# Two adjacency widenings moved into the last projection group: a graph layer in fp32 on one Trainium2 core

## The reference

```python
Wi, Wj = (W[:, :Din], W[:, Din:])
mi = jnp.einsum('bkd,od->bko', x, Wi)
mj = jnp.einsum('bkd,od->bko', x, Wj)
a = adj.astype(x.dtype)
deg = a.sum(axis=1)
out = deg[None, :, None] * (mi + b) + jnp.einsum('ij,bjo->bio', a, mj)
return layernorm(x + out)          # over the last axis, eps 1e-5
```

## Time and profile before

| | |
|---|---|
| median of 3 runs | 1672.72 us (1672.58 to 1673.87) |
| the profiled execution | 1672.83 us |
| its span, first to last instruction | 1670.8 us |
| TensorE matmuls | 1642.1 us busy, 98% of the span |
| ScalarE | 667.4 us, 40% |
| VectorE | 841.9 us, 50% |
| GpSimd | 504.7 us, 30% |
| mean granted TensorE clock | 0.996 of full speed |

### The profile page before, as it was taken

How to read it: one execution, slowest core, us unless ns; L and a number is a source line. 1 busy time by engine, 2 the same in 40 slices (tenths; PEclk the granted TensorE clock), 3 DMA queues, 4 the chain that set the end, 5 groups by cost and what they waited for, 6 DMA issues and landing times.

```text
span 1670.8 us, 24989 instructions
## 1 busy us (share of the span) xinstructions
PE 1642.1 (98%) x7248; PEld 1354.5 (81%) x7248; DVE 841.9 (50%) x1884; ACT 667.4 (40%) x970; POOL 504.7 (30%) x390
## 2 busy tenths in 40 slices
PE   7999999999999999999999999999999999999998
PEld 5878888788887888878888788887888878888786
DVE  7767754455444444445544444444454445444444
ACT  5665435423354323542345332453225433254321
POOL 2541124311343113431134311443114421144211
PEclk8999999999999999999999999999999999999999
DMA  5666522333223332343322332224322333232432
GB/s 171 192 185 214 184 82 91 123 110 104 81 95 119 113 107 75 100 126 105 97 86 95 123 109 94 91 92 132 107 88 88 100 126 107 82 101 82 126 111 71
DMA packets 102698, 187.26 MB, mean 112 GB/s; under 512 B 11408, under 2 KB 11408, under 8 KB 102672
## 3 DMA queue, kind: packets, MB, share of 16 engines
q1 hardware_dynamic: 84528, 153.92, 29.0%
q10 hardware_dynamic: 18144, 33.04, 6.5%
HBM read 119.80 MB, written 67.11 MB: 112 GB/s over the span
## 4 chain that ended last, share of the span: by engine, by line
PE 96%; ACT 1%; DVE 1%; issue 1%; DMA 0%; ACTq 0%; SPq 0%; DVEq 0%
PE agg_ps L329 56%; PE cross_ps L295 14%; PE main_ps L305 13%; PE main_ps L307 13%; ACT adjT L411 1%; DVE W_lo L478 0%; DMA mi_dram<-mi 0%; ACT mj_hi L399 0%; PE deg_ps L314 0%; DMA mi_in<-in_wt 0%; DVE deg_part L523 0%; DVE W_df L480 0%; DVE mj L475 0%; DVE cross L475 0%; ACT cross L395 0%
## 5 line engine op out<-in xcount | busy, mean ns | idle before, releaser
L329 PE MATMUL agg_ps<-mj_hi,adjT 128*128 128x512 f32 x2048 | 798.0, 390 | 10.6 <-ACT adjT L411 9.3
L329 PE MATMUL agg_ps<-mj_lo,adjT 128*128 128x512 f32 x2048 | 796.9, 389 | 0.0
L411 ACT ACTIVATE adjT<-adjT 128x2048 fp32r (+1 forms) x128 | 244.4, 1916 | 548.4 <-PE agg_ps L329 548.4
L329 PEld LDWEIGHTS agg_ps<-mj_hi,adjT 128*128 128x128 f32 x2048 | 384.5, 188 | 93.5 <-POOL mj_lo L252 10.1
L329 PEld LDWEIGHTS agg_ps<-mj_lo,adjT 128*128 128x128 f32 x2048 | 384.4, 188 | 79.6
L305 PE MATMUL main_ps<-W_hi,x_hi 128*128 128x512 f32 x1024 | 399.4, 390 | 0.3 <-DVE mi L509 0.3
L307 PE MATMUL main_ps<-W_lo,x_lo 128*128 128x512 f32 x1024 | 398.9, 390 | 0.0
L258 POOL TENSOR_TENSOR mi_in<-mi_in,bias 128x512 f32<-128x512 f32 x128 | 166.0, 1299 | 664.3 <-DMA mi_in<-mi_dram 664.3
L295 PE MATMUL cross_ps<-W_df,x_df 128*128 128x512 f32 x1024 | 276.4, 392 | 10.0 <-POOL x_df L247 7.7
L252 POOL TENSOR_TENSOR mj_lo<-mj,mj_hi 128x512 f32 (+1 forms) x128 | 173.0, 1351 | 293.5 <-ACT mj_hi L399 293.5
L543 DVE TENSOR_TENSOR r<-agg_ps,r 128x512 f32<-128x512 f32 x128 | 88.5, 692 | 336.2 <-PE agg_ps L329 336.0
(11 more groups left out here) (43 smaller groups left out, 577.5 us busy)
## 6 DMA issues: line engine op xcount, KB each, us to landing
mi_dram<-mi SPq DMA_DIRECT2D x128, 256.0 KB, 2.0
mi_in<-mi_dram SPq DMA_DIRECT2D x128, 256.0 KB, 2.7
r<-in_x SPq DMA_DIRECT2D x128, 256.0 KB, 2.7
out<-r SPq DMA_DIRECT2D x128, 256.0 KB, 2.0
x_raw<-in_xt ACTq DMA_DIRECT2D x126, 256.0 KB, 2.7
adj_in<-in_adjt SPq DMA_DIRECT2D x64, 256.0 KB, 3.1
r<-in_wt SPq DMA_DIRECT2D x4, 256.0 KB, 5.4
x_raw<-in_xt SPq DMA_DIRECT2D x2, 256.0 KB, 3.8
```

Of the source, the lines that this page charges most:

```text
L329: last = nc.tensor.matmul(agg_ps[s][:, :], adjT[s][:, j, :], part[:, j, :], start=(j == 0 and part is mj_hi), stop=(j == NT - 1 and part i ...
L411: nc.scalar.activation(adjT[s][:, :, :], adjT8[:, :, bass.ds(i * P, P)], ACT.Copy).then_inc(adjT_ready, 1)
```

## The change

ScalarE's projection code widens the block of output tile 0 after the first tile's work of the last group (tile 12) and that of output tile 1 after the third tile's (tile 14). The two widenings behind the projection loop are gone. So that the last group is known in the code, ScalarE's group loop makes three turns and the last group is spelled out in all batches. No other engine's code is changed, and no wait is added or taken away.

```diff
                 def proj(g):
+                    last_group = known(g) and g == NG - 1
                     for u in range(GT):
                         t = GT * g + u
                         n = NT * bt + t
-                        if not (final and known(g) and g == NG - 1 and u == GT - 1):
+                        if not (final and last_group and u == GT - 1):
                             parts(n + 1, (u + 1) % 2)
                         take_cross(n, 0)
-                        if not (final and known(g) and g == NG - 1 and u >= GT - 3):
+                        if not (final and last_group and u >= GT - 3):
                             load_x(n + 3, (u + 1) % 2)
                         if zero:
                             cast_chunk(PROJ_CHUNKS * t)
...
                         top_of_mj(n, t)
                         if zero:
                             cast_chunk(PROJ_CHUNKS * t + 1)
-
-                over_groups(act, zero, final, proj)
-                for i in range(2):
-                    widen(i, i, NT if zero else None)
+                        if last_group and u in (0, 2):
+                            widen(u // 2, u // 2, NT if zero else None)
+
+                over_groups(act, zero, True, proj)
```

## The result

The changed kernel takes 1659.89 us (median of 6 executions, 1658.84 to 1660.78) against 1672.90 us (6 executions, 1671.66 to 1673.87) of the kernel before. The ratio is 0.9921, 95% interval 0.991 to 0.9931: 13.0 us less, with 11.5 to 15.1 by the interval. The forecast was 1660.1 us. Four single executions among all that were timed (two of the kernel before and one each of two experiments) took 2370 to 5920 us; the medians given here leave them out.

A forecast was written before the change was run, and what follows sets the result against it. TensorE was taken to bound the kernel, so only its waits could be won: 11.79 us of stops plus 0.8 of restarts, 12.6 us less, takes the median from 1672.72 to 1660.1 us; range 1658.8 to 1663.0.

The forecast's parts named there:

- What the widening cost: TensorE's turn from projection to aggregation: 1.42 us late in six batches, 1.87 and 1.40 in two; 11.79 us to be won.
- The restart: TensorE's second matmul behind each turn's stop comes about 0.10 us late; eight make 0.8 us, bounds 0 and twice that.
- The second widening: Output tile 1 is wanted 7.3 us after tile 0, ready 1.9 us after it: costs nothing before or after.
- The cover on ScalarE: Copies queued behind a widening in a looped batch's projection run 1.1 us late; `x_df` keeps 1.6 us spare.
- `mj`: VectorE's `mj` behind the widening of tile 14 in a looped batch: perhaps 0.1 us late, done before TensorE wants it.
- Batch 0: ScalarE also casts chunks there, so a widening makes `x_hi` 1.65 us late; cost taken as 0, bounds 0 and 1.65.
- What is late next: At the first aggregated tile, VectorE's sum comes 1.4 us behind TensorE's end, with 5.1 us spare.
- Rival 1: At the turn the first matmul waits for the last `mj_lo`: only about 2.7 us won, 1670.0 us; chance 0.04.
- Rival 2: ScalarE falls behind in batch 0; late `x_df` or `mj` stalls TensorE by at most 1.65 us: 1661.7 us; chance 0.06.
- Rival 3: ScalarE's longer loop is fetched again at five jumps back, starts of batches 2 to 6: 1673.6 or 1687 us; chance 0.03.

The follow-up runs named there:

- all_sixteen: The changed kernel, with the aggregation's first matmul waiting for all 16 tiles of `mj_lo` instead of 15: 1670.14 us, ratio 0.9982 to the kernel before.

## Why the prediction was right

- **What the widening cost.** Right in place and size: eight stops, 11.79 us of standing still, all gone, with the batch 7 one among them in spite of its name in the view.
- **The restart** was the term that was sized low. I took 0.10 us, the first interval alone; the batch periods give 0.14, and the made stop 0.17, since the next few intervals are long too. Eight of them are 1.1 us instead of 0.8: 12.9 us in all instead of 12.6, against 13.0 measured. This rests on the traces; the times could not tell 12.6 from 12.9.
- **The second widening costs nothing**: the run with the first alone is as fast as the change.
- **The cover on ScalarE.** Predicted 1.1 us late and 1.6 spare for `x_df`; read 1.0 and 1.72. The rows were of the wrong tile, though: the `x_df` that runs in tile 15 is the next batch's, which the same prediction says is wanted 116 us later, and not at 932.19. The figure held because the widening behind tile 12 delays the same copies by the same time, and there the next tile does want `x_df` at its start. The limit was tried from the other side: 2.8 us late is past it, by 0.07 us for `x_df`. That the expected 1663.5 came as 1663.3 is partly luck, as the trace has 2.7 us for it and not 3.6.
- **`mj`** was to start 0.1 late and did not.
- **Batch 0** was taken at 0 with 1.65 as its bound. `x_hi` of tile 14 is 1.5 us late there, and TensorE does not wait for `x_df`. What it does wait for in that batch is `mi`, which VectorE makes late because it waits for a store of `mi` to DRAM, and that wait differs from run to run (1.4 us in the profile after, 0.3 before). It isn't alone: near 20 us TensorE also waits for `W_df`, for longer in some executions than in others, and behind the longer waits its matmuls are slow (see the last section). These are in the scatter of every time here. They hide little of the 13 us: TensorE's first slot of batch 0's aggregation is 109.39 after and 109.17 before.
- **What is late next** is VectorE's first sum, by 1.2 us instead of the 1.4 predicted, and nobody waits for it.
- **The rivals.** Rival 1 (`mj_lo` takes the wait over) is false as the code stands, and the run that asks for all 16 tiles shows what it would have cost: 10.2 us of the 13.0. Rival 2 did not happen. Rival 3 was tried with a body nearly twice as long and has no sign of itself in the trace.

## What to carry to other kernels

Where two stages follow each other on the engine that bounds the kernel, look at what the helper engine does last in the first stage for the first step of the second: if it does not depend on that stage's last results, it belongs into the idle time before. What may be moved there is found by one subtraction, the time from the end of what is queued behind it to the slot of the bounding engine; here 2.7 us were free, one widening used 1.0 of them, two used them up. And a wait that asks only for what the first step reads (15 of 16 tiles) is what lets the gain come through.

## What the runs showed of the hardware

- TensorE loses 0.14 to 0.17 us beyond the length of a stop of 1.0 to 1.9 us, in the first intervals behind it.
- A stop can cost more than it lasts by the clock. Behind stops of 1.23 to 1.71 us from start to start (all_sixteen) and of 1.63 to 2.10 us (the turns before) no matmul was slow; behind those of 2.05 to 2.39 us three of eight were followed by some 8 matmuls at half the clock, 1.6 us each; behind those of 3.95 to 4.38 us all eight were. Two neighbouring batches with the same stop of 2.39 us differ in it. The wait for `W_df` near 20 us adds to this. In seven of the thirteen profiles it makes a stop of 1.71 to 1.74 us and the matmuls behind are fast; in the other six it makes one of 2.37 to 2.60, and the matmuls behind are slow in all six. So stops of about 2.4 us are followed by the lower level in three of seven cases in one place and in six of six in another. What decides is open.
- The view of waits named three different causes (`adjT` on PE, `mj_lo` on the weight loads, "issue" in batch 7) for one and the same wait.

The second bullet's wait for `W_df`, in the kernel after and in the kernel before, with the four matmuls behind it in 1.20 and in 2.07 us:

```profile
20.80 1.20 PE L295 MATMUL cross_ps<-W_df,x_df 128*128 128x512 f32 x4 [1.23 <-DVE W_df L481]
```
```profile
20.69 2.07 PE L295 MATMUL cross_ps<-W_df,x_df 128*128 128x512 f32 x4 [2.20 <-DVE W_df L480]
```
